# Criss-cross attention: values laid out in device memory by channel tile and image column instead of by pixel

## The chip, the cores and the metric

One core of one Trainium2 chip runs the kernel. The metric is the device time of one execution in microseconds (us). The engines are PE (TensorE), PEld (its weight loads), DVE (VectorE), ACT (ScalarE), POOL (GpSimd) and SP (SyncE, which here only issues DMAs). 16 DMA engines move data between device memory and SBUF.

## The reference, cut to what matters

Input x is [8, 512, 96, 96] in float32. Every pixel attends to all pixels of its image column and its image row:

```python
q = einsum('bchw,oc->bohw', x, Wq) + bq      # 64 channels
k = einsum('bchw,oc->bohw', x, Wk) + bk      # 64 channels
v = einsum('bchw,oc->bohw', x, Wv) + bv      # 512 channels
eH = einsum('bchw,bcpw->bhwp', q, k); eH[h == p] = -inf
eW = einsum('bchw,bchp->bhwp', q, k)
att = softmax(concatenate([eH, eW], axis=3), axis=3)
out = gamma * (einsum('bcpw,bhwp->bchw', v, attH) + einsum('bchp,bhwp->bchw', v, attW)) + x
```

## The kernel before, in words

The loop over the 8 images runs these stages for each image `b`.

**Projection.** The image's 9,216 pixels are cut into 36 blocks of 256 (`BLK`), each block into two tiles of 128 pixels (`PT`). SP loads a block of x (`load_block`, 512 KB in pieces of 1 KB), ACT and DVE split it into a high and a low part, PE makes the values of each tile in three products (L865 to L867), pixels on the partitions and 512 channels in the free dimension. ACT writes the high half of the values as float16 and DVE the low half, into `v_out[k]`, [128 pixels, 4 channel tiles, high/low, 128 channels]; there are four such buffers, so `v_out[k]` comes up again after two blocks. `store_block` (L318) sends each tile to the device-memory tensor `vT`. The tensor is pixel-major: one pixel's 4 x 2 x 128 float16 numbers lie together, 2 KB, so that a tile is 128 pieces of 2 KB, all contiguous. ACT waits for `v_stored[k]` before it overwrites a buffer. `load_next` brings the next image's block, from which DVE takes the maximum for the scales. After two blocks `shift_blocks` moves q and k halves between partitions with three small DMAs. All of these are issued by SP, in program order: for each block `load_block` (of the next round), the two stores, `load_next`; after the second block the three shift DMAs. Six blocks (1,536 pixels, 16 image rows) are one pass of the loop body (`BODY` = 3 double blocks); the loop variable is `j`, the double block in it `d`, the block in that `s`. The row scores are worked in between. Then come the column scores and the softmax factors.

**Attention.** For each of 4 channel tiles (`CT`) there is a column strip (`COL`) and then a row strip (`ROW`), each of 24 groups of 4 image columns or rows. SP loads `v_in[u]`, 6 buffers (`VU`), each of 96 partitions x 8 strips (`VS`) x high/low x 128 channels, 384 KB, for two groups (L384). For `COL` a partition is an image row and takes 8 neighbouring image columns; for `ROW` a partition is an image column and takes 8 neighbouring image rows. In the pixel-major tensor each of these is a piece of 512 B (one pixel, one channel tile). PE multiplies them with the attention weights in 16 matmuls per group (L986) and DVE adds the group to `acc` in SBUF (L827, for tile 0 L841). SP loads a buffer again when PE is done with it (`o_mm`). On the ACT queue, `acc` of tile 2 or 3 is loaded in 12 pieces during the column strip before (L589), and in each row strip the 12 finished pieces of `out` are stored (L559 adds the bias, L563 stores), 384 KB each in rows of 3 KB. For tile 0, the attention weights are first scaled and transposed group by group by POOL, PE, ACT and DVE; the `acc` of tiles 0 and 1 is loaded in two DMAs with rows of 36 KB before it begins. The first six loads of `v_in` go out at the end of the projection.

The waits `v_stored` at the end of the projection stand on SP, ACT and DVE.

Of the kernel before, what the change touches and what calls it, by code (L numbers as in the profile page):

```python
# [7 lines left out]
F16 = mybir.dt.float16  # L8
# [8 lines left out]
P = 128  # L17
# [4 lines left out]
ROW, COL = 0, 1  # L22

def criss_cross_attention(nc, x, wqkT, wvT, bqk, bv, gamma, out):
# [16 lines left out]
    B, C, H, W = x.shape  # L42
    L = H
    assert H == W and C % P == 0 and L <= P
    HW = H * W
    CT = C // P
# [3 lines left out]
    BLK = 256  # L50
    PT = BLK // P
    NB = HW // BLK
    assert NB % 2 == 0 and HW % BLK == 0

    G = 4
# [14 lines left out]
    VS = 2 * G  # L70
    VU = 6
# [5 lines left out]
    x_acc = x.rearrange("b (t c) h w -> b t c (h w)", c=P)  # L77
    out_acc = out.rearrange("b (t c) h w -> b t c (h w)", c=P)

    vT = nc.dram_tensor("v_pixel_major", [B, HW, CT * 2 * P], F16, kind="Internal").ap()  # L80
    vT_load = {
        ROW: vT.rearrange("b (h w) (t a) -> b t w h a", w=W, t=CT),
        COL: vT.rearrange("b (h w) (t a) -> b t h w a", w=W, t=CT),
    }

    base = [(nc.sbuf_base + 63) // 64 * 64]

# [53 lines left out]
    v_out, qk_f32, x_next = [], [], []  # L141
# [54 lines left out]
    with ExitStack() as ctx:  # L196
# [31 lines left out]
        v_stored = [sem(f"v_stored{k}") for k in range(2 * PT)]  # L228
# [56 lines left out]
        def wait_alone(eng, semaphore, value):  # L285

            eng.wait_ge(semaphore, value)
            eng.sem_inc(waits_carried, 1)
# [3 lines left out]
        @block.sync  # L293
        def _(sp):
            for k in range(2 * PT):
                sp.sem_inc(v_stored[k], 16)
            sp.dma_start(wqk_raw[:, :, :], wqkT.rearrange("(t c) o -> c t o", c=P)).then_inc(weights_loaded, 16)
            sp.dma_start(wv_raw[:, :, :], wvT.rearrange("(t c) o -> c t o", c=P)).then_inc(weights_loaded, 16)
            sp.dma_start(bqk_col[:, :], bqk.rearrange("(c u) -> c u", u=1)).then_inc(weights_loaded, 16)
# [15 lines left out]
                    x_next_loaded[s], 16  # L315
                )

            def store_block(b, i, s):  # L318

                for j in range(PT):  # L320
                    k = s * PT + j

                    sp.wait_ge(v_ready, (b * NB + 2 * i) * PT + k + 1 + VTILES)
                    sp.dma_start(
                        vT[b, bass.ds((2 * i + s) * BLK + j * P, P), :],
                        v_out[k][:, :, :, :].rearrange("p t a c -> p (t a c)"),
                    ).then_inc(v_stored[k], 16)

            def shift_blocks(b, i, d):

# [15 lines left out]
            with sp.Fori(0, B) as b:  # L346

                for s in range(2):
                    load_block(b, s, s)  # L350

                wait_alone(sp, out_stored[1], b * (CT // 2 * STORES * 16) + 16)

                wait_alone(sp, o_mm, b * (2 * PH3) + 2 * VU)
                for s in range(2):
                    load_next(b, s, s)

                def double_blocks(j, last):
                    for d in range(BODY):
                        i = j * BODY + d  # L360
                        for s in range(2):
                            more = not (last and d == BODY - 1)
                            if more:
                                load_block(b, 2 * i + 2 + s, s)
                            store_block(b, i, s)
                            if more:
                                load_next(b, 2 * i + 2 + s, s)
                        shift_blocks(b, i, d)

                with sp.Fori(0, NJ - 1) as j:  # L370
                    double_blocks(j, False)
                double_blocks(NJ - 1, True)

                for k in range(2 * PT):
                    wait_alone(sp, v_stored[k], (b + 1) * (NB // 2 * 16) + 16)
                with sp.Fori(0, CT // 2) as tp:
                    for par in range(2):
                        for o in (COL, ROW):
                            with sp.Fori(0, NV) as i:
                                n3 = ((b * CT + tp * 2 + par) * 2 + (1 - o)) * NV + i  # L380
                                for u in range(VU):

                                    sp.wait_ge(o_mm, (n3 * VU + u) * 2 + 2)
                                    sp.dma_start(  # L384
                                        v_in[u][:, :, :, :].rearrange("p s a c -> p s (a c)"),
                                        vT_load[o][b, tp * 2 + par, :, bass.ds((i * VU + u) * VS, VS), :],
                                    ).then_inc(v_loaded[u], 16)

            for k in range(2):
# [65 lines left out]
        def _(act):  # L455
# [13 lines left out]
            def high_v(b, i, s):  # L469
                for j in range(PT):  # L470
                    k = s * PT + j
                    act.wait_ge(v_mm, (b * NB + 2 * i) * PT + k + 1)

                    act.wait_ge(v_stored[k], (b * (NB // 2) + i) * 16 + 16)
                    nc.scalar.activation(  # L475
                        v_out[k][:, :, 0, :], bank[k][:, :].rearrange("p (t c) -> p t c", t=CT), ACT.Copy,
                        scale=scales[:, SCALE_V:SCALE_V + 1],
                    ).then_inc(v_hi_ready, 1)
# [7 lines left out]
            with act.Fori(0, B) as b:  # L486
# [42 lines left out]
                    exp_pair(ROW, p, p % SP)  # L529

                for k in range(2 * PT):
                    act.wait_ge(v_stored[k], (b + 1) * (NB // 2 * 16) + 16)
                for d in range(BODY):
                    act.wait_ge(qk_shifted[d], (b + 1) * (NJ * 3 * 16))
                wait_alone(act, x_next_seen, (b + 1) * NB + BLOCKS)
# [59 lines left out]
        def _(dve):  # L595
# [102 lines left out]
            with dve.Fori(0, B) as b:  # L698
# [63 lines left out]

                for k in range(2 * PT):
                    dve.wait_ge(v_stored[k], (b + 1) * (NB // 2 * 16) + 16)
                for w in range(SP):
                    score_pair(COL, w, w, w - 2 if w > 1 else None)
                    if w < 2:
# [254 lines left out]
```

## Time and profile before

| | |
|---|---|
| Time, median of 3 runs | 4702.74 us (4691.79 to 4703.69) |
| Profiled execution, span from first to last instruction | 4713.9 us |
| PE busy | 3955.7 us (84%) |
| DVE busy | 3102.6 us (66%) |
| ACT busy | 1839.5 us (39%) |
| POOL busy | 706.6 us (15%) |
| DMA queue q1 (issued by SP) | 803.63 MB, 60.7% of 16 engines |
| DMA queue q10 (issued by ACT) | 302.03 MB, 17.7% of 16 engines |
| Moved in all | 1109.71 MB in 1,130,201 packets |
| `v_in` loads | 768 of 384.0 KB, median 8.6 us from issue to landing |
| Stores of the values | 576 of 256.0 KB, median 2.6 us |

The page gives no time of the profiled execution beyond its span. A busy share is an average over the stages of 8 images, whose limits differ; so the busy time by stretch, for one image, says more. The second image runs from about 661 us to about 1237 us of the span. "Granted clock" is the share of TensorE's full clock that it was given. The DMA share is the sum of the times of all packets over the time of 16 engines; packets overlap in an engine, so that it can be above 1. Idle time of an engine that isn't the bottleneck costs nothing.

### The profile page before, as it was taken

To read this page: it belongs to the slowest core of one execution; us is meant where nothing else is said; L and a number is where in the kernel's file an instruction comes from. 1 tells how busy PE (TensorE), PEld (TensorE's weight loads), DVE (VectorE), ACT (ScalarE), POOL (GpSimd) and SP (SyncE) were. 2 spreads that over 40 slices of the span, in tenths; PEclk is the share of its full clock that TensorE was granted. 3 is DMA by queue.
4 is the path that set the end of the run, shared out by engine and by line. 5 is a ranking of instruction groups with operands and counts; after the bars stand their busy time and mean duration, and the time that the engine had idled before them with its cause. 6 is when DMAs were issued, how large, how long until landed. Compare 5 with 4: busy or idle time off the path is not lost.

```text
span 4713.9 us, 122493 instructions
## 1 busy us (share of the span) xinstructions
PE 3955.7 (84%) x39768; PEld 3541.7 (75%) x39768; DVE 3102.6 (66%) x4349; ACT 1839.5 (39%) x3947; POOL 706.6 (15%) x979
## 2 busy tenths in 40 slices
PE   3997689976899778997789977898778987799777
PEld 3887678866788667886778867787677877778777
DVE  6667566675676755767557676576765667667676
ACT  1554135541355313553145521455314543245432
POOL 0113001130011301113011130111301103011120
PEclk9997789977898878988799777897878978799687
DMA  8765987669875797757977489775897758977599
GB/s 265 231 207 197 290 244 229 196 212 297 244 227 176 237 299 235 229 156 256 290 240 230 146 265 290 234 230 157 264 289 230 230 166 256 294 232 228 179 256 284
DMA packets 1130201, 1109.71 MB, mean 235 GB/s; under 512 B 48528, under 2 KB 979856, under 8 KB 1127824
## 3 DMA queue, kind: packets, MB, share of 16 engines
q1 hardware_dynamic: 1044624, 803.63, 60.7%
q10 hardware_dynamic: 85248, 302.03, 17.7%
q8 instruction: 166, 2.72, 0.2%
q14 instruction: 163, 1.34, 0.1%
HBM read 775.16 MB, written 301.99 MB: 229 GB/s over the span
## 4 chain that ended last, share of the span: by engine, by line
PE 53%; DMA 16%; DVE 9%; issue 8%; ACT 5%; SPq 5%; ACTq 1%; DVEq 0%; POOL 0%; POOLq 0%
DMA v_in<-v_pixel_major 15%; PE banks L865 11%; PE banks L986 11%; PE banks L867 11%; PE banks L866 11%; SPq L384 5%; PE banks L886 3%; PE banks L883 3%; DVE x_lo L664 2%; DVE acc L841 2%; PE banks L957 2%; ACT x_hi L467 1%; PE banks L891 1%; DVE nmax L721 1%; ACT prob_row L501 1%
## 5 line engine op out<-in xcount | busy, mean ns | idle before, releaser
L827 DVE SCALAR_TENSOR_TENSOR acc<-banks,scales,acc 128x384 f32 x1152 | 863.0, 782 | 546.9 <-PE banks L986 527.6
L865 PE MATMUL banks<-wv_hi,x_hi 128*128 128x512 f32 x2304 | 923.4, 401 | 150.7 <-DVE x_lo L664 150.4
L866 PE MATMUL banks<-wv_lo,x_hi 128*128 128x512 f32 x2304 | 906.0, 393 | 0.0
L867 PE MATMUL banks<-wv_hi,x_lo 128*128 128x512 f32 x2304 | 904.4, 393 | 0.0
L986 PE MATMUL banks<-prob_col,v_in 96*128 96x96 f16 x12288 | 701.1, 225 | 226.8 <-DMA v_in<-v_pixel_major 164.0
L986 PEld LDWEIGHTS banks<-prob_col,v_in 96*128 96x128 f16 x12288 | 650.5, 109 | 277.4 <-issue 204.8
L986 PE MATMUL banks<-prob_row,v_in 96*128 96x96 f16 x12288 | 713.7, 227 | 169.6 <-DMA v_in<-v_pixel_major 127.5
L986 PEld LDWEIGHTS banks<-prob_row,v_in 96*128 96x128 f16 x12288 | 663.6, 110 | 212.8 <-issue 110.3
L559 ACT ACTIVATE acc<-acc,gbv_col (+1 forms) x384 | 358.6, 934 | 1150.4 <-DVE acc L827 1112.9
L664 DVE TENSOR_TENSOR x_lo<-x_raw,x_hi 128x1024 fp32r<-128x1024 f32 x288 | 396.5, 1379 | 480.1 <-ACT x_hi L467 479.9
L422 POOL TENSOR_TENSOR q_low<-qk_f,q_both 64x256 f32 x288 | 193.6, 672 | 3069.6 <-ACT k_hi L484 3047.9
L865 PEld LDWEIGHTS banks<-wv_hi,x_hi 128*128 128x128 f32 x2304 | 437.8, 190 | 249.5 <-issue 166.4
L672 DVE SCALAR_TENSOR_TENSOR v_out<-banks,scales,v_out 128x512 f16<-128x512 f32 x576 | 422.8, 746 | 215.4 <-ACT v_out L475 215.1
L475 ACT ACTIVATE v_out<-banks,scales 128x512 f16<-128x512 f32 x576 | 385.6, 685 | 375.5 <-PE banks L867 374.7
L867 PEld LDWEIGHTS banks<-wv_hi,x_lo 128*128 128x128 f32 x2304 | 436.7, 190 | 93.3
L866 PEld LDWEIGHTS banks<-wv_lo,x_hi 128*128 128x128 f32 x2304 | 438.1, 190 | 81.3
L883 PE MATMUL banks<-k_hi,q_both 128*96 (+1 forms) x1536 | 340.3, 279 | 42.9 <-POOL k_lo L423 24.5
L467 ACT CAST x_hi<-x_raw 128x1024 fp32r<-128x1024 f32 x288 | 301.5, 1049 | 186.8 <-DMA x_raw<-x 150.3
L624 DVE TENSOR_REDUCE xmax_blk<-x_next 128x1024 f32 (+1 forms) x288 | 348.4, 1210 | 0.0
L886 PE MATMUL banks<-k_lo,q_both 128*96 (+1 forms) x1536 | 339.3, 278 | 0.0
L866 PE MATMUL banks<-x_lo,wqk_hi 128*128 128x256 f32 x1152 | 326.5, 283 | 0.0
L867 PE MATMUL banks<-x_hi,wqk_lo 128*128 128x256 f32 x1152 | 326.3, 283 | 0.0
(84 smaller groups left out, 4766.3 us busy)
## 6 DMA issues: line engine op xcount, KB each, us to landing
v_in<-v_pixel_major SPq DMA_DIRECT2D x768, 384.0 KB, 8.6
x_raw<-x SPq DMA_DIRECT2D x288, 512.0 KB, 4.3
x_next<-x SPq DMA_DIRECT2D x288, 512.0 KB, 3.8
v_pixel_major<-v_out SPq DMA_DIRECT2D x576, 256.0 KB, 2.6
out<-acc ACTq DMA_DIRECT2D x384, 384.0 KB, 5.9
acc<-x ACTq DMA_DIRECT2D x16, 4608.0 KB, 19.3
acc<-x ACTq DMA_DIRECT2D x192, 384.0 KB, 8.9
x_first<-x SPq DMA_DIRECT2D x36, 512.0 KB, 7.5
```

The source lines that it names most:

```text
L467: nc.scalar.copy(x_hi[s][:, :, :], x_raw[s][:, :, :]).then_inc(x_hi_ready, 1)
L475: nc.scalar.activation(v_out[k][:, :, 0, :], bank[k][:, :].rearrange("p (t c) -> p t c", t=CT), ACT.Copy, scale=scales[:, SCALE_V:SCALE_V ...
L559: nc.scalar.activation(acc[k][:, px], acc[k][:, px], ACT.Identity, bias=gbv_col[:, t:t + 1]).then_inc(bias_added, 1)
L664: nc.vector.tensor_tensor(x_lo[s][:, :, :], x_raw[s][:, :, :], x_hi[s][:, :, :].bitcast(F32), ALU.subtract).then_inc(x_split, 1)
L672: nc.vector.scalar_tensor_tensor(out=v_out[k][:, :, 1, :], in0=bank[k][:, :].rearrange("p (t c) -> p t c", t=CT), scalar=scales[:, SCALE_V ...
L827: nc.vector.scalar_tensor_tensor(out=a, in0=out_bank[m % 4], scalar=scales[:, O_FACTOR:O_FACTOR + 1], in1=a, op0=ALU.mult, op1=ALU.add,).t ...
L865: nc.tensor.matmul(dst, s_hi, m_hi, start=(t == 0), stop=False)
L866: nc.tensor.matmul(dst, s_hi, m_lo, start=False, stop=False)
L867: last = nc.tensor.matmul(dst, s_lo, m_hi, start=False, stop=(t == CT - 1))
L883: nc.tensor.matmul(dst[:, g, :], q[:, strip, :], k_h[:, strip, :], start=(o == ROW or g == 0), stop=False)
L886: last = nc.tensor.matmul(dst[:, g, :], q[:, strip, :], k_l[:, strip, :], start=False, stop=(o == ROW))
L986: last = nc.tensor.matmul(dst[:, g, :], v, parts[o][:, h * G + g, c, :], start=(a == 0 and c == 0), stop=(a == 1 and c == 1),)
```

## The change

The tensor `vT` gets the shape [image, channel tile, image column, image row, 256]. For one channel tile and one image column, the 96 image rows' 512 B lie one after the other. A row-strip load takes 8 image rows of one image column per partition, 4 KB in one piece; a column-strip load takes 8 pieces of 512 B that lie 48 KB apart. A store writes, for each pixel, four pieces of 512 B, one per channel tile. Since image row and image column are separate dimensions now, a tile of 128 pixels, which always crosses one border between image rows, is stored by two DMAs (`fragments`), of 96 + 32, 64 + 64 or 32 + 96 pixels. Each tile therefore adds 32 instead of 16 to its semaphore `v_stored[k]`, and all waits on it are doubled to match.

```diff
-    vT = nc.dram_tensor("v_pixel_major", [B, HW, CT * 2 * P], F16, kind="Internal").ap()
+    vT = nc.dram_tensor("v_column_major", [B, CT, W, H, 2 * P], F16, kind="Internal").ap()
     vT_load = {
-        ROW: vT.rearrange("b (h w) (t a) -> b t w h a", w=W, t=CT),
-        COL: vT.rearrange("b (h w) (t a) -> b t h w a", w=W, t=CT),
+        ROW: vT,
+        COL: vT.rearrange("b t w h a -> b t h w a"),
     }
+    vT_store = vT.rearrange("b t w h a -> b h w t a")
+
+    def fragments(px):
+        return [(row, max(px, row * W), min(px + P, (row + 1) * W)) for row in range(px // W, (px + P - 1) // W + 1)]
...
-                sp.sem_inc(v_stored[k], 16)
+                sp.sem_inc(v_stored[k], 32)
...
-            def store_block(b, i, s):
+            def store_block(b, i, s, jj, d):
                 for j in range(PT):
                     k = s * PT + j
+                    px = (2 * d + s) * BLK + j * P
                     sp.wait_ge(v_ready, (b * NB + 2 * i) * PT + k + 1 + VTILES)
-                    sp.dma_start(
-                        vT[b, bass.ds((2 * i + s) * BLK + j * P, P), :],
-                        v_out[k][:, :, :, :].rearrange("p t a c -> p (t a c)"),
-                    ).then_inc(v_stored[k], 16)
+                    for row, first, end in fragments(px):
+                        sp.dma_start(
+                            vT_store[b, jj * (4 * G) + row, first - row * W:end - row * W, :, :],
+                            v_out[k][first - px:end - px, :, :, :].rearrange("p t a c -> p t (a c)"),
+                        ).then_inc(v_stored[k], 16)
...
-                            store_block(b, i, s)
+                            store_block(b, i, s, j, d)
...
-                    wait_alone(sp, v_stored[k], (b + 1) * (NB // 2 * 16) + 16)
+                    wait_alone(sp, v_stored[k], (b + 1) * (NB // 2 * 32) + 32)
...
-                                        vT_load[o][b, tp * 2 + par, :, bass.ds((i * VU + u) * VS, VS), :],
+                                        (vT_load[ROW][b, tp * 2 + par, :, bass.ds((i * VU + u) * VS, VS), :]
+                                         if o == ROW else
+                                         vT_load[COL][b, tp * 2 + par, :, bass.ds((i * VU + u) * VS, VS), :]),
...
-                    act.wait_ge(v_stored[k], (b * (NB // 2) + i) * 16 + 16)
+                    act.wait_ge(v_stored[k], (b * (NB // 2) + i) * 32 + 32)
```

The waits at the end of the projection on ACT and DVE change in the same way as the one on SP.

## Rows read from the trace of the kernel before

**Rows 1.** Busy time by stretch, projection: length, PE, PEld, DVE, ACT, POOL, clock, DMA share, GB/s.
```profile
672.00:932.00 260.00, 252.83 (x1450) 218.15 (x1449) 177.55 (x221) 131.93 (x287) 47.37 (x71) 0.98 0.70 221
```

**Rows 2.** Waits of PE from 680 to 900 us: total us, times, longest.
```profile
PE banks L865 <- DVE x_lo L664: 1.8, 8, 0.2
```

**Rows 3.** Busy time by stretch, tile 0's row strip and later strips.
```profile
1034.00:1061.00 27.00, 23.22 (x474) 21.84 (x473) 24.58 (x41) 12.43 (x21) 6.56 (x8) 1.00 1.07 325
1061.00:1095.00 34.00, 22.57 (x375) 21.50 (x371) 18.57 (x25) 4.55 (x5) 0.00 (x0) 0.75 1.12 283
1095.00:1122.00 27.00, 20.14 (x340) 19.23 (x341) 14.93 (x21) 6.67 (x8) 0.00 (x0) 0.76 1.11 328
...
1157.00:1189.00 32.00, 28.68 (x510) 27.61 (x507) 21.27 (x30) 8.99 (x10) 0.00 (x0) 0.79 1.11 312
1189.00:1211.00 22.00, 19.02 (x405) 17.39 (x403) 18.84 (x27) 5.61 (x6) 0.00 (x0) 1.00 1.17 260
```

**Rows 4.** Waits of PE from 1061 to 1237 us.
```profile
PE banks L986 <- DMA v_in<-v_pixel_major: 33.7, 17, 7.2
```

**Rows 5.** The chain that ended last, 1061 to 1237 us: shares, and its longest piece.
```profile
by line: DMA v_in<-v_pixel_major 49.4%; PE banks L986 25.0%; SPq L384 15.4%; issue 4.9%; DVE acc L827 0.7%; DVE x_lo L664 0.7%; PE banks L865 0.7%; ACT x_hi L467 0.6%; ACT acc L559 0.5%; PE banks L866 0.5%; PE banks L867 0.5%; SPq L383 0.4%
...
1062.81 19.75 DMA v_in<-v_pixel_major
```

**Rows 6.** Busy time by stretch, tile 0's column strip.
```profile
1000.00:1034.00 34.00, 29.50 (x522) 25.93 (x520) 32.00 (x53) 15.05 (x30) 21.35 (x27) 1.00 0.60 169
```

**Rows 7.** DMA from 1186 to 1202 us, when only `v_in` is loaded.
```profile
DMA packets 7445, 3.73 MB, mean 233 GB/s; under 512 B 152, under 2 KB 7445, under 8 KB 7445
```

**Rows 8.** DMA from 25 to 75 us, when only x is loaded, in 1 KB pieces.
```profile
DMA packets 16739, 16.62 MB, mean 332 GB/s; under 512 B 510, under 2 KB 16739, under 8 KB 16739
```

**Rows 9.** DMA from 974 to 985 us, when only whole `acc` rows of 36 KB are loaded.
```profile
DMA packets 144, 4.72 MB, mean 429 GB/s; under 512 B 16, under 2 KB 16, under 8 KB 16
```

**Rows 10.** DMA queues from 1061 to 1237 us: packets, MB, share of 16 engines.
```profile
q1 hardware_dynamic: 51705, 27.21, 68.3%
q10 hardware_dynamic: 8640, 23.60, 39.2%
```

**Rows 11.** The chain from 995 to 1000 us: start, us, what.
```profile
995.21 1.28 PE banks L986 x16
...
996.86 0.68 PE banks L986 x16
```

**Rows 12.** DVE's instructions in order of time, tile 3's column strip: start, us.
```profile
1188.36 6.85 DVE L827 SCALAR_TENSOR_TENSOR acc<-banks,scales,acc 128x384 f32 x8
```

**Rows 13.** Busy time by stretch, while only `v_in` is loaded.
```profile
926.00:935.00 9.00, 9.00 (x53) 8.68 (x52) 5.83 (x11) 5.87 (x25) 0.38 (x1) 0.50 1.14 227
...
1194.00:1201.00 7.00, 6.13 (x128) 5.55 (x128) 6.68 (x10) 0.00 (x0) 0.00 (x0) 1.00 1.19 227
```

**Rows 14.** Line 324, the store's issue on SP: ns min/median/max.
```profile
L324 SPq DMA_DIRECT2D v_pixel_major<-v_out x576: 332/368/1389, 78.1 to 4402.8; - x192
```

**Rows 15.** Waits of SP from 680 to 900 us.
```profile
SPq L324 <- DVE v_out L672: 62.2, 41, 2.8
SPq L314 <- DVE xmax_blk L624: 30.8, 30, 1.2
SPq L333 <- POOL k_lo L423: 11.2, 15, 0.8
```

**Rows 16.** DMA from 680 to 900 us: the queue, and issues with median us to landing.
```profile
q1 hardware_dynamic: 44182, 50.58, 71.3%
...
x_raw<-x SPq DMA_DIRECT2D x31, 512.0 KB, 4.2
v_pixel_major<-v_out SPq DMA_DIRECT2D x60, 256.0 KB, 2.4
```

**Rows 17.** SP's instructions at the end of the projection: start, us.
```profile
911.15 7.04 SPq L324 DMA_DIRECT2D v_pixel_major<-v_out  x4
920.64 0.51 SPq L333 DMA_DIRECT2D q_both<-q_low  x1
```

More of the change, by code:

```diff
@@ L531, in _ @@
                 for k in range(2 * PT):
-                    act.wait_ge(v_stored[k], (b + 1) * (NB // 2 * 16) + 16)
+                    act.wait_ge(v_stored[k], (b + 1) * (NB // 2 * 32) + 32)
                 for d in range(BODY):
@@ L764, in _ @@
                 for k in range(2 * PT):
-                    dve.wait_ge(v_stored[k], (b + 1) * (NB // 2 * 16) + 16)
+                    dve.wait_ge(v_stored[k], (b + 1) * (NB // 2 * 32) + 32)
                 for w in range(SP):
```

## The prediction

> **What bounds the kernel now.** I read the page first, then busy times by stage of the second image, then PE's waits and the chain in the longest DMA-bound stage, then the DMA packets by window.
>
> An image has two stages that matter. In the projection stage (672 to 932 us) PE is busy 252.83 of 260 us at the full clock (0.98) while the DMA share is 0.70 [rows 1]; in 220 us of it PE waits 1.8 us [rows 2]. It is bound by PE. In channel tiles 1 to 3 of the attention stage (1061 to 1237 us, 176 us) the DMA share is 1.11 or more in the strips shown up to 1211 us, and the granted clock falls to 0.75 or 0.76, so PE sits at its lower level (1.2 GHz) for half of the time [rows 3]. PE waits 33.7 us for `v_in` there [rows 4], and by the chain, DMA of `v_in` makes 49.4% and its issue on SP another 15.4% [rows 5]. The tile-0 pass before it is different: from 1000 to 1034 us DVE is busy 32.00 of 34 us at a DMA share of 0.60 [rows 6].
>
> **What a packet costs.** Each `v_in` load is 384 KB in 768 pieces of 512 B. Where such pieces run alone they reach 3.73 MB in 16 us, 233 GB/s [rows 7]: 512 B / (233/16 GB/s) = 35 ns per piece and engine, 393,216 B / 233 GB/s = 1.69 us per load. Pieces of 1 KB alone reach 332 GB/s over 50 us, with a lull at the end of it [rows 8], pieces of 36 KB alone 429 GB/s [rows 9]. I price the 3 KB pieces of `acc` and `out` at 429 GB/s, 0.917 us per 384 KB. Check on the stage itself: it moves 27.21 MB on q1, practically all `v_in`, and 23.60 MB on q10 [rows 10]: 117 + 55 = 172 us of the 176. By design of the loops the same sum is 72 loads x 1.69 + 24 `acc` loads x 0.917 + 36 stores x 0.917 = 121.7 + 55.0 = 176.7 us. The stage is DMA-bound to within its error.
>
> **Row loads: the gain.** In the new layout the 8 image rows that a partition takes for one image column lie together: 96 pieces of 4 KB instead of 768 of 512 B. The trace of before has no 4 KB piece. From below: the 36 KB rate, 393,216 B / 429 GB/s = 0.917 us per load; from above, 1.69 us, as now. I take 0.917, because the stage sum already works with that price for 3 KB pieces, the nearest size. That is 0.77 us less per row load; 3 tiles x 12 row loads = 36 per image: 27.8 us less DMA work in the stage, 176.7 -> 148.9 us.
>
> How much shows? The next bound is compute: at the full clock PE takes 0.68 us for a group of 16 matmuls, at the half clock 1.28 us [rows 11]; DVE adds column groups at 6.85/8 = 0.86 us each [rows 12]. Full-clock floor: 3 x 24 x 0.86 + 3 x 24 x 0.68 = 62 + 49 = 111 us, 38 us under the new DMA sum, so DMA stays the bound. By strips of 24 groups, column strips of tiles 1 and 2 stay at 12 x 1.69 + 12 x 0.917 = 31.3 us of DMA, those of tile 3 at 20.3 (about DVE's 20.6), and the row strips go from 31.3 to 22.0. That last number is above PE's 16.3 at the full clock and under its 30.7 at the half clock. So part of the saving is lost where the clock is low while a row strip has its data, and in tile 3, where DVE leaves no room to catch up. I take 80%: 22 us per image. The row strip of tile 0 has 12 loads with 9 us less DMA work too, but DVE is busy 24.58 of its 27 us [rows 3]; it earns nothing itself, and only helps tile 1 to start with its buffers full, where one DMA piece of the chain is now 19.75 us long [rows 5]. That is inside my 80%. Over 8 images: -176 us.
>
> The Trainium skill, "DMA: Bandwidth & Descriptors", section Specifications, says that a transfer needs at least 512 B for line rate. By that rule 512 B pieces would already run as fast as 4 KB pieces, a row load would save nothing, and the time would be that of rival B below. Here [rows 7, 9] say 233 against 429 GB/s, so the trace doesn't agree.
>
> **Column loads: same count and size, other pitch.** 768 pieces of 512 B as before, but a partition's 8 pieces lie 48 KB apart (2 KB before) and neighbouring partitions 512 B apart (192 KB before). Before, the row loads step 192 KB within a partition and 2 KB between partitions, the reverse of the column loads. Column loads (926 to 935 us) run at 227 GB/s, and so do the loads from 1194 to 1201 us, by their place in the queue mostly those of the row strip [rows 13]. Pitch is not seen. Price: 0, with a margin of +-10% on 1.69 us for the range: 36 column loads x 0.17 = 6 us per image, +-49 us in all.
>
> **Stores.** Each 128-pixel tile was one DMA of 128 pieces of 2 KB. Now it is two DMAs (a tile always crosses one image-row border: 96+32, 64+64 or 32+96 pixels) with 512 pieces of 512 B in all. DMA work per tile: before 262,144 B / 429 GB/s = 0.61 us at least; after 1.13 us at the 233 GB/s of reads. No 512 B write to device memory is in the trace; from below it is at the old 0.61, from above at 1.13 x 2. I take 1.13, +0.52 us per tile. 72 tiles per image: +37 us of DMA work in 260 us where the share is 0.70, so about 0.84: hidden behind PE, which has 1.8 us of waits in 220 [rows 2]. If that cover were gone, it would be 37 x 8 = 300 us.
>
> The second DMA of a tile costs SP one more issue, 0.368 us [rows 14], with its address work about 0.5: two tiles per block, so 1.0 us more per block of 260/36 = 7.2 us. SP has room: it waited 62.2 + 30.8 + 11.2 us in 220 us for DVE and POOL [rows 15], 3.4 us per block. Behind the extra stores are queued `load_next`, the three shift DMAs and the next `load_block`; x loads land in 4.2 us, stores in 2.4 us [rows 16], and a `v_out` buffer comes up again only after two blocks, 14 us. At the end of the projection the four last stores are issued by 911.15 + 7.04 = 918.2 us, and the shift that PE waits for goes at 920.64, held by POOL [rows 17]: one more issue behind each store fits in. All semaphore sums double with the increments; no new wait. I take +1 us per image for jitter: +8 us.
>
> The same page of the Trainium skill, section Latency and other measured facts, reports that HBM rows at pitches of 4 MiB and more, powers of two, ran at half rate. By it the four pieces of a pixel, 4.5 MiB apart, could be at risk, and a store would cost twice, 2.3 us per tile (an estimate). The x blocks are read with exactly this tile pitch (128 channels x 36 KB) and reach the rate of [rows 8], so the trace speaks against it, for reads.
>
> **Sum.** -176 + 8 = -168 us. Against the span of the profiled execution, 4713.9 us (the page shows no time outside it), that is 4546 us. The median of the runs is 4702.74, 11.2 us under that span; so 4535 us for the median. Likeliest case: chance 0.66, own range 4480 to 4600 (100% to 55% of the DMA saving, column loads +-5%).
>
> **Rivals.**
> A. Clock and overlap take half. The row strips stay near the half clock, where PE needs 30.7 us per strip against DMA's 22.0 [rows 11]. For: the clock is 0.75 in this stage now. Against: it is at 1.00 from 1189 to 1211 us, as soon as PE is fed [rows 3]. With half the saving: 8 x 14 - 8 = 104 us, 4600 us. Chance 0.12.
> B. The row loads bring nothing: the row access is still cut into 512 B pieces, or 4 KB pieces run no faster, as by the page's first rule. For: every piece of `v_in` now is 512 B. Against: the 36 KB packets show that a long run goes in one piece [rows 9]. Time: 4703 + 8 = 4711 us. Chance 0.06.
> C. Column loads at the 48 KB pitch run 10 to 20% slower, 6 to 12 us per image: 4535 + 49 to 98, about 4610 us. It would eat the whole gain from 22/36 = 0.6 us per load, 36% slower. Chance 0.07.
> D. Slower than before: scattered 512 B writes are so dear that the projection turns DMA-bound. Room: (1 - 0.713) x 220 us / 60 stores [rows 16] = 1.05 us per tile. Above 0.61 + 1.05 = 1.66 us per tile (52 ns per piece) PE begins to wait for x; from 1.66 + 168/576 = 1.95 us per tile (61 ns per piece) on, the whole kernel is slower. At 3 us per tile: (3 - 1.66) x 576 = 772 - 168, about 5300 us; at twice the read price, 2.26 us: 346 - 168 = +178, 4880 us. For: no such write is in the trace. Against: reads at this tile pitch pay nothing. Chance 0.09.
>
> **Chances and range.** A difference under 0.3% (14 us) can't be told from none. Faster: likeliest 0.66 + A 0.12 + C 0.05 = 0.83. Same: B 0.04 + C 0.01 = 0.05. Slower: D 0.09 + B 0.02 + C 0.01 = 0.12. For 8 in 10 the range goes from 4455 (the whole saving in tiles 1 to 3, and tile 0's too, with column loads slightly quicker) to 4650 (A and C).
>
> **What would show it.** q1 packets: 576 x 384 more for the stores and 384 x 672 fewer for the row loads, with 9,216 more of the second DMAs' completions 28 thousand fewer in all. Row loads land sooner than column loads; the row strips, now 27 and 32 us [rows 3], shrink by 5 to 9, the column strips keep theirs, the clock in the stage rises from about 0.75. The projection keeps its 260 us with a DMA share of 0.80 to 0.88. Wrong would be: a projection over 265 us with PE waiting for x (D); `v_in` row issues with 768 pieces (B); column strips longer than 36 us (C); a clock still at 0.75 beside a DMA share well under 1.0 (A).

## The result, and the profile after

The median of four runs is 4646.86 us (4636.81 to 4655.39) against 4698.4 us for four runs of the kernel before, 51.5 us less. The ratio measured over the runs is 0.987, 95% interval 0.9848 to 0.9892, which is 61 us. Five more runs (e8 below) gave 0.9875 (0.9856 to 0.9894) and medians 65 us apart. So the change is faster by 1.1% to 1.4%, 50 to 65 us, where 168 us were forecast. The profiled execution has a span of 4635.0 us, 78.9 us under that of before.

A correction to the forecast's stretches comes first. They were read 11 us late against the strips: tile 1's column strip of the second image begins at 1050 us, and DVE adds the last group of tile 3's row strip at 1225.5 us. So the window from 1061 to 1237 us ends with 11 us behind the image's last group, and the rows named as strips straddle two. Its sums hardly change (175 us for 176), but the two kernels have to be compared strip by strip. Busy time by stretch, kernel before, cut at the strips: the projection, then column, row, column, row, column, row of tiles 1 to 3; columns as in [rows 1]:

```profile
655.00:917.00 262.00, 259.80 (x1453) 223.16 (x1454) 177.43 (x217) 130.13 (x266) 47.01 (x70) 0.99 0.69 224
1050.00:1084.00 34.00, 20.61 (x390) 19.93 (x387) 21.42 (x25) 1.02 (x2) 0.00 (x0) 0.82 1.10 299
1084.00:1110.50 26.50, 22.68 (x391) 21.59 (x390) 14.83 (x24) 10.29 (x11) 0.00 (x0) 0.78 1.13 309
1110.50:1146.50 36.00, 23.67 (x400) 22.75 (x396) 21.59 (x24) 0.94 (x1) 0.00 (x0) 0.72 1.12 273
1146.50:1178.00 31.50, 22.85 (x372) 21.87 (x373) 14.65 (x24) 11.03 (x12) 0.00 (x0) 0.72 1.09 316
1178.00:1200.00 22.00, 20.56 (x417) 19.12 (x415) 20.91 (x25) 0.20 (x1) 0.00 (x0) 0.94 1.16 260
1200.00:1225.50 25.50, 20.80 (x340) 19.33 (x337) 13.77 (x24) 10.29 (x11) 0.00 (x0) 0.72 1.07 321
```

The same stretches of the changed kernel:

```profile
642.50:904.50 262.00, 260.07 (x1449) 223.06 (x1450) 175.34 (x215) 129.33 (x266) 47.11 (x70) 0.99 0.78 223
1037.50:1068.50 31.00, 20.46 (x382) 19.76 (x380) 20.96 (x24) 0.94 (x1) 0.00 (x0) 0.76 1.09 289
1068.50:1098.00 29.50, 22.27 (x389) 21.34 (x387) 14.83 (x25) 11.22 (x12) 0.00 (x0) 0.79 1.05 348
1098.00:1131.00 33.00, 25.52 (x393) 24.36 (x391) 22.23 (x25) 0.00 (x0) 0.00 (x0) 0.69 1.07 264
1131.00:1159.50 28.50, 20.35 (x382) 19.38 (x379) 14.76 (x24) 11.23 (x12) 0.00 (x0) 0.82 1.05 343
1159.50:1182.50 23.00, 20.22 (x401) 18.76 (x398) 21.30 (x24) 0.00 (x0) 0.00 (x0) 0.93 1.13 262
1182.50:1200.50 18.00, 16.33 (x355) 15.22 (x352) 14.07 (x24) 8.89 (x10) 0.00 (x0) 1.00 1.02 346
```

The projection keeps its 262 us and PE its 260; only its DMA share grows, 0.69 to 0.78. Rates in the row strips rise from 309 to 321 up to 343 to 348 GB/s, not to 429. In this image tile 1's row strip is longer than before (29.5 us for 26.5), tile 2's shorter (28.5 for 31.5) and tile 3's much shorter (18 for 25.5); over the images only the last remains. The DMA share stays above 1 and the clock of the first four strips at 0.69 to 0.82. Mean over images 2 to 8, in us, a strip from its first group to the next strip's first group (the last one to its last group), taken from the starts of DVE's groups (for the last two rows, of PE's matmuls too) in the two traces:

| | before | after |
|---|---|---|
| tile 0 | 61.9 | 60.6 |
| tile 1, column strip and row strip | 33.8, 27.7 | 31.9, 27.7 |
| tile 2, column strip and row strip | 35.4, 29.3 | 33.2, 29.4 |
| tile 3, column strip and row strip | 24.3, 24.4 | 24.1, 16.8 |
| tiles 1 to 3, first group to last | 174.9 | 163.2 |
| last group to the next image's first matmul | 8.8 | 12.2 |
| projection, first matmul to last | 262.6 | 262.4 |

Over 8 images: 8 x (1.3 + 11.7) = 104 us gained, 7 x 3.4 = 24 us given back, 80 in all, about the difference of the spans. Of the 11.7 us, 7.6 come in the last row strip and 4.1 in the two column strips beside which `acc` is loaded. The row strips of tiles 1 and 2, whose loads were changed too, keep their length. Why the gain falls this way isn't settled.

**Where the row loads are slow.** DMA of the changed kernel from 1180 to 1188 us, when only row loads run, answers to [rows 7]:

```profile
DMA packets 598, 2.10 MB, mean 262 GB/s; under 512 B 83, under 2 KB 83, under 8 KB 598
```

So 4 KB pieces alone move at 262 GB/s, little over the 233 of 512 B pieces.

The new loads also keep SP less. Its time to issue one `v_in` load (ns min/median/max), before and after:

```profile
L384 SPq DMA_DIRECT2D v_in<-v_pixel_major x768: 317/1157/10714, 342.2 to 4694.4; - x192
L391 SPq DMA_DIRECT2D v_in<-v_column_major x768: 317/318/7746, 342.8 to 4617.4; - x192
```

SP's issue makes 10.9% of the chain from 1037 to 1213 us, where it made 15.4% [rows 5]. No run separates this from the transfers themselves.

**Where time is given back.** The chain at the end of the second image, changed kernel: start, us, what.

```profile
1200.03 0.94 ACT acc L568
...
1201.78 0.94 ACT acc L568
...
1203.52 0.94 ACT acc L568
...
1205.24 3.80 issue
1209.24 1.05 ACT x_hi L476
```

ACT adds the bias to a piece (L568), waits for its own result, and issues the store, every 1.74 us; a piece takes PE less, 2 x 0.68 us at the full clock [rows 11]. DVE starts its last group at 1200.4, ACT goes on until 1205. Before, the same place reads:

```profile
1222.56 2.76 PE banks L986 x32
1225.45 0.63 DVE acc L827
1226.21 0.94 ACT acc L559
1227.32 0.34 ACTq L563
1227.93 3.60 issue
```

One ACT piece comes after the last group, and PE was the late one.

PE's waits from 1037 to 1213 us, changed kernel, answer to [rows 4]:

```profile
PE banks L995 <- DMA v_in<-v_column_major: 32.4, 22, 8.1
PE banks L874 <- DVE x_lo L673: 11.4, 1, 11.4
```

The wait for `v_in` is about as large as before (32.4 us for 33.7); the one for the next image's `x_lo` was 8.9 us.

### The profile page after: what moved, and what is told of

It reads as the page before. It is cut to its first block, busy times and chain, and to the rows that moved or that the text cites. A ratio compares the mean times of both kernels' runs of the same rounds, so it can differ in the third digit from the quotient of the medians.

```text
span 4635.0 us, 124229 instructions
## 1 busy us (share of the span) xinstructions
PE 3895.6 (84%) x39768; PEld 3483.0 (75%) x39768; DVE 3091.3 (67%) x4349; ACT 1838.1 (40%) x3947; POOL 708.0 (15%) x979
## 4 chain that ended last, share of the span: by engine, by line
PE 52%; DMA 17%; DVE 10%; issue 9%; ACT 7%; SPq 2%; ACTq 2%; DVEq 1%; POOL 0%; POOLq 0%
DMA v_in<-v_column_major 15%; PE banks L874 11%; PE banks L875 11%; PE banks L876 11%; PE banks L995 10%; PE banks L895 3%; PE banks L892 3%; ACT acc L568 2%; DVE acc L850 2%; DVE x_lo L673 2%; SPq L391 2%; ACT x_hi L476 2%; ACT prob_row L510 1%; PE banks L900 1%; DVE nmax L730 1%
## 5 line engine op out<-in xcount | busy, mean ns | idle before, releaser
L995 PE MATMUL banks<-prob_col,v_in 96*128 96x96 f16 x12288 | 714.8, 227 | 255.8 <-DMA v_in<-v_column_major 203.1
L995 PEld LDWEIGHTS banks<-prob_col,v_in 96*128 96x128 f16 x12288 | 664.1, 110 | 308.0 <-issue 243.2
L568 ACT ACTIVATE acc<-acc,gbv_col (+1 forms) x384 | 358.6, 934 | 1076.0 <-DVE acc L836 1027.7
L995 PE MATMUL banks<-prob_row,v_in 96*128 96x96 f16 x12288 | 641.6, 215 | 91.0 <-DMA v_in<-v_column_major 52.1
L995 PEld LDWEIGHTS banks<-prob_row,v_in 96*128 96x128 f16 x12288 | 595.2, 103 | 130.8 <-DVE acc L836 80.9
L476 ACT CAST x_hi<-x_raw 128x1024 fp32r<-128x1024 f32 x288 | 301.7, 1050 | 226.5 <-DMA x_raw<-x 188.0
L892 PE MATMUL banks<-k_hi,q_both 128*96 (+1 forms) x1536 | 340.1, 279 | 43.7 <-POOL k_lo L432 24.5
```

What stands on the lines that cost most here:

```text
L476: nc.scalar.copy(x_hi[s][:, :, :], x_raw[s][:, :, :]).then_inc(x_hi_ready, 1)
L568: nc.scalar.activation(acc[k][:, px], acc[k][:, px], ACT.Identity, bias=gbv_col[:, t:t + 1]).then_inc(bias_added, 1)
L892: nc.tensor.matmul(dst[:, g, :], q[:, strip, :], k_h[:, strip, :], start=(o == ROW or g == 0), stop=False)
L995: last = nc.tensor.matmul(dst[:, g, :], v, parts[o][:, h * G + g, c, :], start=(a == 0 and c == 0), stop=(a == 1 and c == 1),)
```

## The experiments

The theory after the first look, PORT: a transfer over 96 of the 128 partitions loads the ways into SBUF unevenly, so that it runs at some 260 GB/s whatever its pieces. Its rival, PITCH: device memory is slow at 48 KB between partitions. The ratios below are to the kernel before, run beside each. The kernels that only move data (e1, e7, e11) ran once each; the pattern of row loads in e1 and e7 gave 262 GB/s both times, that of new column loads 244 and 232. So differences of some 5% between patterns of 512 B pieces say nothing.

### Patterns alone (e1)

A kernel that only moves data, each pattern 24 transfers over six buffers, all landed before the next begins. In short:

```python
buf[u][0:96, :] <- x_flat[96 partitions, pitch 48 KB, 4 KB]     # also 52 KB, also contiguous
buf[u][0:128, :] <- x_flat[128 partitions, pitch 48 KB, 4 KB]   # also 64 partitions
buf[u][0:96, 8, 512 B] <- new column, old column, old row pattern; also 128 partitions
out <- src   # 36 tiles as 128 x 2 KB, or as two DMAs of 512 B pieces
...          # 128 x 3 KB as acc; 24 loads beside 12 acc pieces
```

> This kernel leaves the whole attention out and only moves data, one pattern after the other, with all of a pattern's transfers landed before the next begins. It asks why 4 KB row pieces move at about 260 GB/s alone in the changed kernel (and not at 429). Theory PORT (96 of 128 partitions spread unevenly over the ways into SBUF): 96 x 4 KB gives 250 to 280 GB/s at a pitch of 48 KB, of 52 KB and contiguous alike, and 128 x 4 KB at the 48 KB pitch gives over 380 GB/s. Theory PITCH (device memory is slow at 48 KB between partitions): 48 KB slow for 96 and for 128 partitions, 52 KB or contiguous over 350 GB/s. For 512 B pieces PORT expects over 300 GB/s with 128 partitions against 233 with 96, and no difference between the old and new column pitches. For the stores: 128 x 2 KB near 400 GB/s; two DMAs of 512 B pieces at 230 to 300 GB/s if they cost what reads do. Row loads beside acc loads: PORT expects both together at 240 to 300 GB/s, beside acc stores 350 to 420 GB/s.

Rates over a whole pattern, its bytes by the time from its first packet to its last landing: 96 x 4 KB 262 GB/s at a pitch of 48 KB, 270 at 52 KB, 265 contiguous; 128 x 4 KB 396; 64 x 4 KB 207; 128 x 3 KB, as `acc`, 372. In pieces of 512 B over 96 partitions: new columns 244, old columns 228, old rows 239; over 128 partitions 288. DMA inside single patterns: 96 x 4 KB at 48 KB, 96 x 4 KB contiguous, 128 x 4 KB, 64 x 4 KB, 128 x 3 KB, 512 B (new columns) over 96 and over 128, then the stores in 2 KB and in 512 B pieces, each with its queue:

```profile
DMA packets 2595, 9.12 MB, mean 268 GB/s; under 512 B 369, under 2 KB 369, under 8 KB 2595
...
DMA packets 2559, 8.98 MB, mean 272 GB/s; under 512 B 367, under 2 KB 367, under 8 KB 2558
...
DMA packets 3160, 11.52 MB, mean 411 GB/s; under 512 B 349, under 2 KB 349, under 8 KB 3160
...
DMA packets 1661, 5.44 MB, mean 209 GB/s; under 512 B 334, under 2 KB 334, under 8 KB 1661
...
DMA packets 3216, 8.77 MB, mean 399 GB/s; under 512 B 361, under 2 KB 361, under 8 KB 3216
...
DMA packets 17125, 8.59 MB, mean 246 GB/s; under 512 B 344, under 2 KB 17125, under 8 KB 17125
...
DMA packets 22451, 11.32 MB, mean 290 GB/s; under 512 B 337, under 2 KB 22451, under 8 KB 22451
...
DMA packets 4609, 8.39 MB, mean 381 GB/s; under 512 B 512, under 2 KB 512, under 8 KB 4609
q1 hardware_dynamic: 4609, 8.39, 102.4%
...
DMA packets 18282, 8.82 MB, mean 221 GB/s; under 512 B 1072, under 2 KB 18281, under 8 KB 18281
q1 hardware_dynamic: 18281, 8.82, 86.4%
```

For 4 KB pieces the pitch is nothing, the number of partitions nearly all. The 3 KB pieces of `acc` take 25.4/24 = 1.06 us per 384 KB alone, not 0.917.

The stores took 24.9/36 = 0.69 us per tile before and 43.5/36 = 1.21 after, +0.52 us, the forecast's number. But that is elapsed time. With the scattered stores the queue's share is 0.86, and SP issues the 72 DMAs with 0.04 us between two, so the DMA engines weren't full. Times their shares, the tiles cost 0.71 and 1.04 us of DMA work, +0.34 us, 24 us per image. The projection's share rose by 0.09 of 262 us, the same 24 us.

Row loads beside other traffic, 24 loads and 12 pieces of 384 KB: 52.0 us beside loads of `acc` (272 GB/s), 41.3 beside stores (343); new column loads 54.5 and 50.9; 128 x 4 KB beside loads of `acc` 43.7. Three expectations were missed: over 300 GB/s for 512 B over 128 partitions (288), 350 or more for row loads beside stores (343), 230 or more for scattered stores (217).

### A pitch of 52 KB in the kernel (e2)

```diff
-... [B, CT, W, H, 2 * P], F16, kind="Internal").ap()
+... [B, CT, W, H + 8, 2 * P], F16, kind="Internal").ap()[:, :, :, 0:H, :]
```

> The changed kernel with 8 unused image rows behind each image column in the values' tensor, so that columns lie 52 KB apart and not 48 KB. Theory PITCH: row loads rise from 260 towards 400 GB/s, 8 us per image less, about 4580 us. Theory PORT: nothing changes, 4647 us within 0.3%.

4640.87 us, ratio 0.985 (0.9817 to 0.9883): the changed kernel's time. PITCH, which expected about 4580 us, falls.

### The change without its 4 KB pieces (e3)

```diff
-... [B, CT, W, H, 2 * P], F16, kind="Internal").ap()
+... [B, CT, W, H, 3 * P], F16, kind="Internal").ap()[:, :, :, :, 0:2 * P]
```

> The changed kernel with 256 unused bytes behind each 512 B of the values' tensor: stores and column loads keep their count and size of pieces, but a row load is again 768 pieces of 512 B. It is the change without the 4 KB pieces. If the pieces' size brought the whole gain and the scattered stores cost nothing, the time is that of before, 4698 us within 0.3%. If the stores cost something that the gain hides, it is above: each us per image adds 8 us. If the gain came from another source (the order of the addresses), it stays near 4647 us.

4706.45 us, ratio 0.9985 (0.9969 to 1.0001). The queue of SP moved the same bytes in more packets than ever:

```profile
q1 hardware_dynamic: 1275024, 803.66, 65.0%
```

Tiles 1 to 3 take 175.3 us per image, as before. So the scattered stores, the second DMA per tile and the column loads' larger pitch cost nothing that shows, and the whole gain comes with the row pieces' size: faster transfers, shorter issues on SP, or both.

### The store issued behind the next bias (e4, e5)

```diff
-                    with act.Fori(0, NV) as i:
-                        for u in range(VU):
-                            store_rows(t, i * VU + u)
+                    if t < CT - 1:
...
+                        continue
+                    for c in range(STORES):
+                        add_bias(t, c)
+                        if c:
+                            store_added(t, c - 1)
+                    store_added(t, STORES - 1)
```

> The changed kernel with one edit on ACT: in tile 3's row strip the store of a piece is issued after the bias activation of the next piece, so that the issue runs beside the activation. In the changed kernel the last row strip's stores follow each other every 1.74 to 1.87 us (activation 0.94, then wait and issue), slower than the two DVE groups a piece needs (1.36 us), and from the last group to the next image's first matmul 12.2 us pass against 8.8 before. Theory HANDBACK (the ACT chain of bias and store takes back 3.4 us per image): the gap falls back to 9 or below, 24 to 30 us less in all, about 4620 us. Rival (the gap is made by the DMA backlog of stores and x loads): no change from 4647 us within 0.3%.

> The same edit on the kernel before, where PE ends the last row strip later than the stores could go. HANDBACK: nothing or at most 4 us gained, 4698 us within 0.3%. The rival, that the edit helps by itself wherever it stands: about the same gain as on the changed kernel.

`add_bias` and `store_added` are the two halves of `store_rows`; tiles 1 and 2 keep their loop. On the changed kernel 4625.97 us, ratio 0.9836 (0.9817 to 0.9855); on the kernel before 4711.88 us beside 4708.97, ratio 1.0011 (0.9994 to 1.0028). The changed kernel without the edit ran on another chip (0.987 and 0.9875), so the edit is worth 16 to 21 us after the change, by ratios or by medians, and nothing before it. The chain at the end of the second image now reads, with the edit on the changed kernel:

```profile
1189.47 8.33 DMA v_in<-v_column_major
1197.92 1.55 PE banks L1008 x32
1200.26 0.94 ACT acc L566
1201.84 5.32 issue
1207.34 1.05 ACT x_hi L476
```

ACT keeps up, and the last group waits for `v_in` again. The mean gap to the next image's first matmul is 10.1 us (12.2 without the edit, 8.8 in the kernel before): 7 x 2.0 = 14 us; tiles 1 to 3 are 0.6 us shorter per image. HANDBACK holds, though not for all of the 3.4 us: 1.4 us stay. The stretch that the profile calls "issue" is longer, 5.32 us here for 3.80; what fills it isn't settled.

### Row loads cut to an eighth (e6)

```diff
+                                    some = VS if o == COL else 1
                                     sp.dma_start(
-                                        v_in[u][:, :, :, :].rearrange("p s a c -> p s (a c)"),
...
+                                        v_in[u][:, 0:some, :, :].rearrange("p s a c -> p s (a c)"),
+                                        vT_load[o][b, tp * 2 + par, :, bass.ds((i * VU + u) * VS, some), :],
```

> The changed kernel with each row load cut to the first of its eight image rows (96 x 512 B, an eighth of the bytes; the other seven rows' values are left out, the buffers keep older numbers). It prices DMA work in the row strips: 1.3 us per row load, 47 us per image in tiles 1 to 3, go away. Theory DMA-BOUND: row strips of tiles 1 and 2 fall from 28 us to what stores, compute or clock allow (16 to 21 us, ACT's bias and store chain being 12 x 1.75 = 21), column strips by 3 us from fuller buffers: 25 to 30 us per image, 4430 us. Theory COMPUTE (the row strips are already held by PE at half clock or by ACT): they stay above 25 us, over 4560 us.

4490.22 us, ratio 0.9549 (0.9526 to 0.9571). Busy time by stretch, second image: tile 1's row strip, tile 2's column and row strips:

```profile
1046.50:1063.60 17.10, 17.10 (x393) 17.10 (x391) 14.84 (x25) 8.14 (x9) 0.00 (x0) 0.97 0.75 249
1063.60:1100.60 37.00, 24.65 (x384) 23.52 (x381) 21.76 (x25) 3.09 (x4) 0.00 (x0) 0.70 0.99 287
1100.60:1117.80 17.20, 17.20 (x390) 17.20 (x388) 14.70 (x24) 8.37 (x9) 0.00 (x0) 0.95 0.72 237
```

The row strips fall from 28 to 17 us, PE busy throughout at nearly the full clock: they were bound by the transfers, and COMPUTE falls. But the column strip between them grows from 33 to 37 us (mean of images 2 to 8: 33.2 to 37.6). In the program ACT issues an `acc` piece after every second column group, so those loads stay in the column strips however short the row strips get. That this makes the growth is argued, not tested. Of 47 us less DMA work per image, tiles 1 to 3 show 163.2 - 142.2 = 21 us, 45%, and the gap at the image's end grows to 13.6 us. That is why the time lay between the two expectations, a little nearer to the first.

### Cuts of the 96-partition load (e7)

In short:

```python
edges = (0,) + cuts + (96,)     # (), (32,), (64,), (48,), (16,), (80,), (32, 64), (16, 48)
for a, e in zip(edges, edges[1:]): buf[u][a:e, :] <- x_flat[a:e, pitch 48 KB, 4 KB]
```

> Moves data alone, as the first pattern kernel; the attention is left out. It asks whether the 96-partition load of 4 KB pieces can be cut so that its partitions spread better: [0:32]+[32:96], [0:64]+[64:96], 48+48, 16+80, 80+16, three and more cuts, and other ranges of partitions. 
Uncut 262 GB/s; with cuts at 32, 64, 48, 16, 80, (32, 64) and (16, 48): 245, 240, 227, 235, 240, 240, 247. Into partitions 32 to 127: 266; 16 to 111: 273. 112 partitions 280, 32 alone 206, 16 alone 115, and 96 partitions in pieces of 2 KB 251. Column loads of 512 B pieces: uncut 232, cut at 32 241, at 64 226, within the spread. No cut helps the row loads; the idea that neighbours' collisions could be cut away falls for one cut. The cut at (32, 64) gave 246 in e1. With two cuts SP never waits for a buffer, so its own pace of issuing may limit those. The same holds for 16 partitions, where the DMA share is only 0.81. DMA inside the patterns of 32, 16 and 112 partitions:

```profile
DMA packets 1001, 2.74 MB, mean 211 GB/s; under 512 B 332, under 2 KB 332, under 8 KB 1001
...
DMA packets 682, 1.40 MB, mean 117 GB/s; under 512 B 341, under 2 KB 341, under 8 KB 682
...
DMA packets 2866, 10.27 MB, mean 285 GB/s; under 512 B 360, under 2 KB 360, under 8 KB 2866
```

32 and 64 partitions have the same rate, 206 and 207 GB/s, and 128 have 396. The Trainium skill, "SBUF — State Buffer", section Door 1: The DMA port swizzle, says that the rate depends on how many of 16 ports the partitions reach: 0 to 31 and 0 to 63 reach the same eight, 0 to 127 all 16. With that these three rates agree. By the table of the same page of the Trainium skill 0 to 95 reach all 16 ports as well, eight of them with 8 partitions and eight with 4. So the count of ports alone would give 96 partitions the rate of 128, and 262 doesn't agree with it. An estimate from that table and the 396 GB/s: if a port with 8 partitions sets the time, 96 partitions get 3/4 of 396, 297 GB/s, and 112 get 7/8, 346; measured are 262 and 280. Uneven ports can therefore be why 96 are slower than 128, but not all of it. What makes the rest is open.

### Row loads of 128 partitions (e8, e9, e10)

```diff
-    vT = nc.dram_tensor("v_column_major", [B, CT, W, H, 2 * P], F16, kind="Internal").ap()
+    vW = nc.dram_tensor("v_column_major", [CT * W + P - W, H, 2 * P], F16, kind="Internal").ap()
+    vT = vW[0:CT * W, :, :].rearrange("(t w) h a -> t w h a", t=CT)
...
+                                    if o == ROW:
+                                        sp.dma_start(
+                                            v_in[u][:, :, :, :].rearrange("p s a c -> p s (a c)"),
+                                            vW[bass.ds((tp * 2 + par) * W, P), bass.ds((i * VU + u) * VS, VS), :],
+                                        ).then_inc(v_loaded[u], 16)
...
```

The `v_in` buffers grow to 128 partitions, PE reads partitions 0 to 95 of them, and the padding is set to zero once at the start.

> The changed kernel once more, beside the kernel before and the next two on the same chip, so that they can be compared directly: 0.987 of before.

> The changed kernel with row loads of 128 image columns instead of 96: the 32 more belong to the next channel tile (or to a padding of zeros behind the last) and land in partitions that no matmul reads. The tensor holds one image instead of eight. A load moves 512 KB instead of 384. Theory PORT: 128 partitions fill all ways into SBUF alike, and alone 512 KB take 1.32 us against 1.50 for 384 KB (396 and 262 GB/s in the pattern kernel); beside acc loads, 24 loads and 12 acc pieces took 43.6 us against 52.0. Per image 36 x 0.18 to 0.35 us less DMA work, of which about half showed when row loads were cut to an eighth: 3 to 6 us per image, about 4615 us. Rival BYTES (the DMA engines' total is what counts): a third more bytes in row loads, 36 x 0.3 us more, 20 to 80 us slower than 4647.

> The edit of the run with wide row loads and the one with the store issued behind the next activation, together. If they add up: 25 to 50 us less for the first, 20 for the second, about 4590 us. If the last row strip is short already and the first edit only gives its gain to the ACT chain, the two give more than their sum.

| | median us | ratio, 95% interval |
|---|---|---|
| changed kernel again (e8) | 4645.91 | 0.9875 (0.9856 to 0.9894) |
| wide row loads (e9) | 4614.01 | 0.9793 (0.978 to 0.9806) |
| wide row loads, store behind (e10) | 4604.29 | 0.9774 (0.9761 to 0.9787) |

The three ran on one chip. Row loads with a third more bytes make the kernel 32 us faster: PORT expected 4615, BYTES 4667 to 4727. By the two traces, whose spans are 25 us apart, 2.9 us per image are gained in tiles 1 to 3 (160.3 for 163.2) and 1.2 in the gap behind them (11.0 for 12.2), and 0.5 lost in tile 0. Row strips of tiles 1 and 2 with wide loads:

```profile
1071.70:1096.90 25.20, 17.95 (x385) 17.10 (x382) 14.84 (x25) 11.22 (x12) 0.00 (x0) 0.90 1.04 395
...
1128.40:1156.10 27.70, 18.83 (x360) 17.20 (x358) 14.54 (x24) 11.22 (x12) 0.00 (x0) 0.89 1.04 401
```

They move 395 and 401 GB/s at a share of 1.04, where the changed kernel moves 348 and 343 at 1.05. The store edit adds 10 us and not 20, so the two don't add up: with wide loads the last row strip is longer (18.7 us against 16.8, mean of images 2 to 8, first group to last), and ACT is less behind. e10 is the fastest kernel here that computes everything. One thing was changed along with the width, the tensor holding one image instead of eight; what that does alone was not run, so the 32 us belong to both.

### Patterns in company (e11)

```python
12 v_in loads (SP) beside 12 pieces of 384 KB on ACT: accs <- x, then out <- accs
```

> Moves data alone: 12 v_in loads of one pattern on SP beside 12 pieces of 384 KB on ACT, first as acc loads (into SBUF), then as stores (out of SBUF). The attention is left out. PORT expects, beside acc loads: old and new row loads of 96 partitions about 27 us each (both kinds go into SBUF), wide ones 24 or less; beside stores: old rows 25, new rows 21, wide rows 20 or less. Column patterns old and new alike, 27 beside acc loads and 25 beside stores; wide columns no faster, since 8 x 128 pieces of 512 B cost 1.82 us alone against 1.61. BYTES expects the wide patterns a fifth to a third slower than the narrow ones.

Us for 12 loads and 12 pieces together, one pass each:

| loads | beside loads of `acc` | beside stores |
|---|---|---|
| old rows, 96 x 8 x 512 B | 34.2 | 30.0 |
| new rows, 96 x 4 KB | 32.6 | 24.8 |
| wide rows, 128 x 4 KB | 28.6 | 28.1 |
| old columns | 34.9 | 30.0 |
| new columns | 33.7 | 30.8 |
| wide columns | 34.7 | 33.2 |

Beside `acc` loads the order is as PORT expects; the times are 4 to 8 us longer than expected. Beside stores the wide rows are 3 us slower than the narrow ones, not quicker: PORT misses there. The narrow ones already move 380 GB/s with the stores and the wide ones 390, so the extra bytes cost time, as BYTES has it. New rows beside `acc` loads, new rows beside stores, wide rows beside `acc` loads:

```profile
DMA packets 3067, 9.42 MB, mean 289 GB/s; under 512 B 384, under 2 KB 384, under 8 KB 3067
...
DMA packets 3074, 9.46 MB, mean 380 GB/s; under 512 B 384, under 2 KB 384, under 8 KB 3072
...
DMA packets 3454, 11.01 MB, mean 385 GB/s; under 512 B 382, under 2 KB 382, under 8 KB 3454
```

Two streams into SBUF take about the sum of their times alone: new rows 36.0/2 + 25.4/2 = 30.7 us against 32.6, wide rows 15.9 + 12.7 = 28.6 against 28.6. New rows in and stores out take 24.8. With these prices the stage sums to 2 x 34.9 + 3 x 30.0 + 20.8 = 180.6 us before and 2 x 33.7 + 3 x 24.8 + 19.4 = 161.2 after (tile 3's column loads alone, half of their e1 patterns); the traces have 174.9 and 163.2. The sum gets the stage to 3%, but not strip by strip: it puts 15.6 of its 19.4 us of gain into the row strips, and those of tiles 1 and 2 kept their length. For wide rows it would be 171, but the trace has 160.3. The sum doesn't hold that a row strip's first loads run beside the last `acc` pieces of the column strip, where the wide ones win 4 us per 12. Whether that makes the 32 us was not tested.

## Why the prediction was wrong

- **What bounds the kernel: right.** The projection is bound by PE and tiles 1 to 3 by the transfers (e6). The stretches were 11 us off. That hid that column strips beside `acc` loads take longer than row strips beside stores (33.8 and 35.4 us against 27.7 and 29.3), where the forecast's sum gave both 31.3: one price for all company.
- **Price of a row load: wrong, and the step that failed.** The forecast took 0.917 us because the stage sum worked with that price for 3 KB pieces. Those pieces go to 128 partitions, these to 96. Alone a row load takes 36.0/24 = 1.50 us, so a load gains 0.15 us on the old rows (39.5/24 = 1.65) alone, 0.13 beside `acc` loads ((34.2 - 32.6)/12) and 0.43 beside stores ((30.0 - 24.8)/12), instead of 0.77. The 3 KB pieces themselves take 1.06 us alone. Beside old row loads one of them adds 1.20 us as a load of `acc` ((34.2 - 19.75)/12) and 0.85 as a store ((30.0 - 19.75)/12), where the stage sum had 0.917 for both. It came out within 1% with two prices wrong, so it didn't prove the price that was then used. With 0.43 for 0.77 the forecast's own terms give 8 x 36 x 0.43 x 0.8 - 8 = 91 us.
- **80% of it showing: not tested at that size.** By e11's prices 19.4 us less work per image, 11.7 shown, 60%; by e6, 45% of 47.
- **Column loads at no cost: right** (e3; 244 and 232 GB/s against 228 for the old pattern).
- **Stores hidden: right, their price in part by luck.** The projection keeps its 262 us, and PE's waits in 220 us of it are 1.9 against 1.8 [rows 2]. The elapsed time per tile alone rose by 0.52 us as forecast, but with the DMA engines not full; the DMA work rose by 0.34. So the share is 0.78 where the forecast had 0.84. SP's extra issue shows nowhere in the projection. Rival D is out.
- **The end of an image: not in the forecast.** It asked what is late next for the strips but not for the store chain on ACT behind the last one: 3.4 us per image given back, 24 us in all, where it had 1 us of jitter per image. e4 gets back 16 to 21 us, e5 nothing before the change.
- **The rules of the Trainium skill.** "DMA: Bandwidth & Descriptors", section Specifications, has 512 B as enough for line rate (rival B). That isn't borne out: 512 B and 4 KB differ by a tenth at 96 partitions (239 and 262 GB/s) and by over a third at 128 (288 and 396). The half rate at pitches of 4 MiB and more, section Latency and other measured facts, didn't come: a store took 1.21 us per tile, not 2.3. But that section measured powers of two and 4.5 MiB is none, so the rule itself wasn't tried.
- **Rivals.** B's other reason is out: the count of q1's packets fell by 27,648, as worked out. A came nearest with 4600 us, but not by its mechanism. Its sign was a clock at 0.75 beside a DMA share well under 1, and the share stayed at 1.02 or above; with fewer bytes the clock was there at once (e6: 0.97).
- **The range: luck.** 4647 us lies inside 4455 to 4650, at the very end that stood for A and C, and neither came. The lower end doesn't follow from its terms either: 4703 - 8 x (27.8 + 9) + 8 is 4417.
- **The signs.** The row strips were to shrink by 5 to 9 us each; the last one shrank by 7.6, the others by nothing. The column strips were to keep their length; two of them lost 2 us. The clock from tile 1 to tile 3 rose only from 0.78 to 0.81.

## What to carry to other kernels

Price a transfer by rows with its number of partitions and its company, not only its piece size: here 96 partitions got 262 GB/s in pieces of 4 KB, and 128 got 396. If a load covers 96 partitions and its pieces are large, reading 32 more for nothing can be faster beside other loads, and slower beside stores; try it. When a sum of prices meets a measured time, measure each price alone before using one of them elsewhere. When a strip gets shorter, look at what chain each engine runs after its last group.

## What the runs showed of the hardware that I had not expected

Pieces of 4 KB at 64 partitions ran at 207 GB/s, at 32 at 206. 24 loads of 512 KB over 128 partitions landed sooner than 24 of 384 KB over 96: 31.8 against 36.0 us. 12 loads over 96 partitions and 12 pieces of 384 KB together took 32.6 us when both went into SBUF (289 GB/s) and 24.8 when one went out (380). Writes of 512 B scattered over 4.5 MiB pitches ran at 217 GB/s with the DMA engines at a share of 0.86; reads of 512 B pieces over as many partitions ran at 288.
